# Attention B: a PSUM bank for the values, two weight sets, outputs around the values, and probability squares moved through DRAM

## The chip, the cores and the metric

One Trainium2 chip; the kernel runs on one of its cores. The metric is the device time of one execution in microseconds, the median of several runs. Engines are named as the profile does: PE (TensorE) with its weight loads PEld, DVE (VectorE), ACT (ScalarE), POOL (GpSimd), and SP (SyncE), which here only issues DMAs (SPq in the rows).

## What is computed

Four residual sublayers on x of 8 x 256 tokens x 256 features, all fp32: attention A, a mixture of experts, attention B, and the experts again. The change touches attention B alone:

```
q, k, v = x @ wq, x @ wk, x @ wv        # 16 heads of 128
q, k    = rope(q), rope(k)
s       = (q * mult) @ (k * mult).T     # 256 x 256 per head and sequence, causal mask
p       = softmax(s)
r       = (p @ v) @ wo                  # summed over heads
x       = x + r                         # x had a layernorm ahead of q, k, v
```

## The kernel before, in words

**Precision.** A product in "three parts" (`matmul3`, L114 to L116) splits both factors into a high part (rounded to fp32r) and a low remainder, and runs low x high, high x low, high x high into one accumulation. So every weight has an upper copy made by ACT (`split_hi`, `split_wo`: `wh`, `woh`) and a lower copy made by DVE (`split_lo`, `split_wo`: `wl`, `wol`). In the kernel before there is one set of these four tiles, overwritten for each head pair.

**Tiling.** The 2048 tokens are 4 slots (`s`) of 512 tokens (two sequences each); the 16 heads are 8 head pairs (`it`). A slot of a head pair is the unit of the pipeline, 32 in all, numbered n = 4 it + s. Each has 4 "pairs" j (a head and a sequence), and `step(it, s, j)` is written out by hand for each engine: PE, ACT and DVE run the same 16 steps per head pair in their own fixed order. `moved(it, s, j, by)` names the pair that lies `by` steps later. PE's order in a slot, with n the current slot:

- every j: `scores` of the pair 7 steps ahead, `mix` (probabilities times values) of the pair before
- j = 0: `project` 2 and 3 of slot n+2 (second head's q and k), then `output` 3 of slot n-2
- j = 1: `project_values` 0 of slot n+1
- j = 2: `output` 0 of slot n-1, then `project` 0 and 1 of slot n+3
- j = 3: `project_values` 1 of slot n+1, then `output` 1 and `output` 2 of slot n-1

**PSUM banks.** Scores alternate over banks 0 and 1; `PROJ(i)` is bank 3 or 4 for projection i even or odd; `MIX` has 5 and 6; `OUT` is bank 7 alone. Bank 2 is not used in this stage. The values are projected into `PROJ(0)` and `PROJ(1)` too, so `project_values` waits until the projection before it in that bank was multiplied by the cosines (DVE, `rope`, L378) and copied with swapped halves (ACT, `swap_b`, L372 and L373), and a later `project` waits until the values were copied out (`take_values`, ACT).

**Outputs.** `output(.., t)` (one tile of 128 tokens, both heads, in `OUT`) waits until `add_out` of the tile before it (DVE, two L1235) has read the bank. DVE's order at j = 2 is `row_max` (L1211), `invert`, `turn_squares` (L1221), `add_out` 0, `rope` 0, `rope` 1; at j = 3 it is `row_max`, `invert`, `turn_squares`, `add_out` 1, `mixed_lo`. `add_out` 2 and 3 of a slot follow at j = 0 and 1 of the slot after.

**Rotation.** After `swap`, POOL multiplies by the sines (L378) and adds (L1345), two instructions per projection; `scores` waits for that.

**Weights.** ACT's `split_wo(it)` is at s = 1, j = 0 and DVE's at s = 1, j = 1 of the head pair that uses it from s = 1, j = 2 on. `split_hi` and `split_lo` of the next head pair are at s = 1, j = 1 (q and k, after their last use) and s = 3, j = 0 (values).

**Squares.** `probs` are turned in 32 x 32 squares by DVE (`turn_squares`) within each block of 32 partitions; to be a full transpose the squares must then change partition blocks. SP does this in `move_squares(n)` with 16 DMAs from SBUF to SBUF per slot, each of 32 rows of 1536 bytes. It starts when the four pairs of slot n were turned, which is at j = 1 of slot n-1, and `mix` of slot n, pair 0, which is at j = 1 of slot n, waits for all 16.

PE and ACT run head pairs 1 to 6 in a hardware loop of one head pair; DVE's and SP's steps are written out.

Of the kernel before, what the change touches and what calls it, by code (L numbers as in the profile page):

```python
# [6 lines left out]
ALU = mybir.AluOpType  # L7
# [842 lines left out]
def attention_b(nc, c, name, w_qkv, w_out, stage, wo_stage, stage_in, wo_in, own_norm, norm, ahead):  # L850
# [7 lines left out]
    LANDED = 16 * 16  # L858
    with ExitStack() as ctx:
        sem = lambda n: ctx.enter_context(nc.semaphore(f"{name}_{n}"))  # L860
        sb = lambda n, s, d=F32: ctx.enter_context(nc.sbuf_tensor(f"{name}_{n}", s, d))
        wh, wl = sb("wh", [P, 3, KD, 2 * P], F32R), sb("wl", [P, 3, KD, 2 * P], F32R)
        woh, wol = sb("woh", [P, 2, D], F32R), sb("wol", [P, 2, D], F32R)
# [11 lines left out]
        squares_done, landed = sem("squares_done"), [sem("landed_even"), sem("landed_odd")]  # L875
# [4 lines left out]
        PROJ = lambda i: c.ps[:, 3 + i % 2, :]  # L880
        MIX = lambda h: c.ps[:, 5 + h, :]
# [8 lines left out]
        pair_no = lambda it, s, j: (it * NG + s) * PAIRS + j  # L890
        is_first = lambda it: isinstance(it, int) and it == 0
# [7 lines left out]
        @block.sync  # L899
        def _(sp):  # L900
            def move_squares(n):

                sp.wait_ge(squares_done, PAIRS * (n + 1))
                after(sp, pv_done, PAIRS * (n - 1))
                for qs in range(4):
                    for ks in range(4):
                        sp.dma_start(probsT[ks * SQ:(ks + 1) * SQ, n % 2, qs], squares[qs * SQ:(qs + 1) * SQ, n % 2, ks]).then_inc(landed[n % 2], 16)

            fetch(sp, ahead)
            for it in range(HP):  # L910
                for s in range(NG):
                    move_squares(slot_no(it, s))
                    if s == 0 and it + 1 < HP:

                        sp.wait_ge(w_lo, 2 * (it + 1))
                        sp.dma_start(stage[:], w_qkv[it + 1]).then_inc(stage_in, 16)
                    if s == 3 and it + 1 < HP:

                        sp.wait_ge(wo_lo, it + 1)
                        sp.dma_start(wo_stage[:], w_out[it + 1]).then_inc(wo_in, 16)  # L920

        @block.tensor
        def _(pe):
            def project(it, s, i):
# [5 lines left out]
                early = isinstance(n, int) and n < 2  # L930
                if i == 0:

                    if early:
                        after(pe, rope_read, 3 * n)
                        after(pe, swap_done, 3 * n)
                    else:
                        pe.wait_ge(values_done, 2 * n - 3)
                elif i == 3 and not early:

                    pe.wait_ge(values_done, 2 * n - 2)  # L940
                else:

                    before = (0, 4 * n, 4 * n + 1, 4 * n + 2)[i]
                    after(pe, rope_read, before)
                    after(pe, swap_done, before)
                col = slice((i // 2) * P, (i // 2) * P + P)
                g = slice(s * G, (s + 1) * G)
                for k in range(KD):
                    ins = matmul3(nc, PROJ(i), (wh[:, i % 2, k, col], wl[:, i % 2, k, col]), (c.xh[:, k, g], c.xl[:, k, g]), k == 0, k == KD - 1)
                ins.then_inc(proj_ready, 1)  # L950

            def project_values(it, s, i):
# [12 lines left out]
                for t in range(2):  # L965
                    tok = slice(s * G + (2 * i + t) * P, s * G + (2 * i + t + 1) * P)
                    for k in range(KD):
                        ins = matmul3(nc, PROJ(i)[:, t * 2 * P:(t + 1) * 2 * P], (c.xh[:, k, tok], c.xl[:, k, tok]), (wh[:, 2, k, :], wl[:, 2, k, :]), k == 0, k == KD - 1)
                ins.then_inc(vproj_ready, 1)
# [31 lines left out]
            def output(it, s, t, bank=OUT, before=1):  # L1001
# [14 lines left out]
                for h in range(2):  # L1016
                    ins = matmul3(nc, bank[:, h * D:(h + 1) * D], (mh[:, s % 2, h, tok], ml[:, s % 2, h, tok]), (woh[:, h, :], wol[:, h, :]), True, True)
                ins.then_inc(out_ready, 1)

            def step(it, s, j):  # L1020
# [12 lines left out]
                if j == 0 and not (first and s <= 1):  # L1033
                    output(*moved(it, s, 0, -2 * PAIRS)[:2], 3)
                if j == 2 and not (last and s >= 1):
                    project(*moved(it, s, 0, 3 * PAIRS)[:2], 0)
                    project(*moved(it, s, 0, 3 * PAIRS)[:2], 1)
                if j == 3 and not (first and s == 0):
                    output(*moved(it, s, 0, -PAIRS)[:2], 2)
                if last and s == 3 and j == 0:  # L1040

                    pe.wait_ge(values_done, 2 * NG * HP)
                    norm_turn(nc, c, norm, pe, 0, norm_banks)

            def head_pair(it):
                for s in range(NG):
                    for j in range(PAIRS):
                        step(it, s, j)

            for i in range(4):  # L1050
                project(0, 0, i)
            norm_turn(nc, c, own_norm, pe, 2, own_banks)
            project(0, 1, 0)
            project(0, 1, 1)
            scores(0, 0, 0)
            scores(0, 0, 1)
            project(0, 1, 2)
            project(0, 1, 3)
            scores(0, 0, 2)
            scores(0, 0, 3)  # L1060
            project_values(0, 0, 0)
# [3 lines left out]
            project(0, 2, 0)  # L1065
            project(0, 2, 1)
            scores(0, 1, 0)
            scores(0, 1, 1)
            project_values(0, 0, 1)
# [3 lines left out]
            head_pair(0)  # L1073
            with pe.Fori(1, HP - 1) as it:
                head_pair(it)
            head_pair(HP - 1)
            mix(*LAST)
            output(HP - 1, NG - 2, 3, S(0), 3)
            norm_turn(nc, c, norm, pe, 1, norm_banks)
            output(HP - 1, NG - 1, 0, S(1), 3)  # L1080
            output(HP - 1, NG - 1, 1, OUT, 3)
            output(HP - 1, NG - 1, 2, S(0), 3)
            output(HP - 1, NG - 1, 3, S(1), 3)
# [3 lines left out]
        def _(act):  # L1087
            def split_hi(it, part):
                act.wait_ge(stage_in, 16 * (it + 1))

                if part == 0:
                    after(act, proj_ready, 4 * NG * it)
                else:
                    after(act, vproj_ready, 2 * NG * it)
                nc.scalar.copy(flat(wh[:, parts[part]]), flat(stage[:, parts[part]])).then_inc(w_hi, 1)

            def split_wo(it):
                act.wait_ge(wo_in, 16 * (it + 1))

                after(act, out_ready, TG * NG * it)  # L1100
                nc.scalar.copy(woh[:], wo_stage[:]).then_inc(wo_hi, 1)
# [16 lines left out]
            def take_values(it, s, i):  # L1118
# [4 lines left out]
                nc.scalar.copy(values[:, s % 2, 2 * i:2 * i + 2, :], PROJ(i).rearrange("p (t d) -> p t d", t=2)).then_inc(values_done, 1)  # L1123
# [8 lines left out]
            def step(it, s, j):  # L1132
                first, last = is_first(it), is_last(it)
                if s == 1 and j == 1 and not last:
                    split_hi(it + 1, 0)
                if exists(it, s, j, LEAD):
                    exps(*moved(it, s, j, LEAD))
                if s == NG - 1 and j == 0 and not last:
                    split_hi(it + 1, 1)
# [12 lines left out]
                if s == 1 and j == 0:  # L1152
                    split_wo(it)
# [3 lines left out]
            def head_pair(it):  # L1157
                for s in range(NG):
                    for j in range(PAIRS):
                        step(it, s, j)  # L1160

            split_hi(0, 0)
            split_hi(0, 1)
# [19 lines left out]
            head_pair(0)  # L1183
            with act.Fori(1, HP - 1) as it:
                head_pair(it)
            head_pair(HP - 1)
# [5 lines left out]
        def _(dve):  # L1192
            def split_lo(it, part):
                dve.wait_ge(w_hi, 2 * it + part + 1)
                nc.vector.tensor_tensor(flat(wl[:, parts[part]]), flat(stage[:, parts[part]]), flat(wh[:, parts[part]]).bitcast(F32), ALU.subtract).then_inc(w_lo, 1)

            def split_wo(it):
                dve.wait_ge(wo_hi, it + 1)
                nc.vector.tensor_tensor(wol[:], wo_stage[:], woh[:].bitcast(F32), ALU.subtract).then_inc(wo_lo, 1)
# [37 lines left out]
            def step(it, s, j):  # L1237
# [3 lines left out]
                if s == 1 and j == 1 and not last:  # L1241
                    split_lo(it + 1, 0)
# [7 lines left out]
                if j == 0:  # L1250
                    if s == NG - 1 and not last:
                        split_lo(it + 1, 1)
# [12 lines left out]
                if s == 1 and j == 1:  # L1265
                    split_wo(it)
# [16 lines left out]
            split_lo(0, 0)  # L1283
            norm_rows(nc, c, own_norm, dve, 2)
            split_lo(0, 1)
# [27 lines left out]
            row_max(0, 1, 2)  # L1313
            for it in range(HP):
# [493 lines left out]
```

## Time and profile before

| | us |
|---|---|
| median of 3 runs | 1719.42 (1718.95 to 1720.47) |
| the profiled execution | 1721.0, its span 1719.2 |
| stage of attention B in the span | about 745 to 1430 |

| engine | busy, share of the span | instructions |
|---|---|---|
| PEld | 1334.2 us, 78% | 9400 |
| DVE | 1112.3 us, 65% | 2592 |
| ACT | 816.6 us, 48% | 2012 |
| POOL | 632.2 us, 37% | 550 |

PE, the first engine of the page, has its row further down. Busy time of matmuls overlaps from one to the next, since the end of a matmul is modelled; the start-to-start distance of the rows of a timeline is the better measure of what a matmul costs. The idle time in brackets stands on the first instruction after a gap, with the event that ended it.

### The profile page before, as it was taken

To read this page: it belongs to the slowest core of one execution; us is meant where nothing else is said; L and a number is where in the kernel's file an instruction comes from. 1 tells how busy PE (TensorE), PEld (TensorE's weight loads), DVE (VectorE), ACT (ScalarE), POOL (GpSimd) and SP (SyncE) were. 2 spreads that over 40 slices of the span, in tenths; PEclk is the share of its full clock that TensorE was granted. 3 is DMA by queue.
4 is the path that set the end of the run, shared out by engine and by line. 5 is a ranking of instruction groups with operands and counts; after the bars stand their busy time and mean duration, and the time that the engine had idled before them with its cause. 6 is when DMAs were issued, how large, how long until landed. Compare 5 with 4: busy or idle time off the path is not lost. (4 is left out here: it accounts for less than half of the span.)

```text
span 1719.2 us, 28814 instructions
## 1 busy us (share of the span) xinstructions
PE 1550.6 (90%) x9400; PEld 1334.2 (78%) x9400; DVE 1112.3 (65%) x2592; ACT 816.6 (48%) x2012; POOL 632.2 (37%) x550
## 2 busy tenths in 40 slices
PE   6699999999799999968888888989898878999998
PEld 4588888887688888857777777878787776888887
DVE  6577777777765555664766666666666678655555
ACT  3366666666433333236555555555555633233332
POOL 2676676776100000045555454445454520000000
PEclk9899999999899999989999999999999999999999
DMA  2100000000101000002121221212121210000001
GB/s 90 52 16 16 16 15 15 15 0 1 43 19 37 19 18 0 1 37 56 48 58 49 60 54 45 61 37 63 35 71 35 52 40 31 25 19 19 18 1 49
DMA packets 35232, 57.61 MB, mean 34 GB/s; under 512 B 9280, under 2 KB 29760, under 8 KB 35136
## 3 DMA queue, kind: packets, MB, share of 16 engines
q1 hardware_dynamic: 35136, 56.48, 11.4%
q8 instruction: 42, 0.69, 0.2%
q14 instruction: 54, 0.44, 0.1%
HBM read 29.18 MB, written 2.10 MB: 18 GB/s over the span
## 5 line engine op out<-in xcount | busy, mean ns | idle before, releaser
L378 POOL TENSOR_TENSOR ab_swapped<-ab_swapped,const 128x512 f32<-128x512 f32 x128 | 163.7, 1279 | 289.9 <-ACT ab_swapped L373 289.9
L1626 DVE TENSOR_TENSOR f_hidden<-ps,f_silu 128x512 f32<-128x512 f32 x128 | 87.7, 690 | 202.0 <-PE ps L116 201.9
L1516 ACT ACTIVATE f_silu<-ps 128x512 f32<-128x512 f32 x128 | 76.3, 598 | 283.0 <-PE ps L116 282.9
L114 PE MATMUL ps<-xh,f_wl 128*128 128x512 f32 x512 | 203.2, 397 | 1.5 <-DVE f_hidden L1626 1.5
L115 PE MATMUL ps<-xl,f_wh 128*128 128x512 f32 x512 | 202.8, 396 | 0.0
L116 PE MATMUL ps<-xh,f_wh 128*128 128x512 f32 x512 | 202.6, 396 | 0.0
L1115 ACT ACTIVATE ab_probs<-ab_probs,ab_negmax 128x128 f32<-128x128 f32 (+1 forms) x256 | 114.5, 448 | 151.7 <-DVE ab_negmax L1211 149.1
L1235 DVE SCALAR_TENSOR_TENSOR x<-ps,ab_inv,x 128x256 f32<-128x256 f32 x256 | 121.2, 474 | 88.3 <-PE ps L116 82.0
L1345 POOL TENSOR_TENSOR ab_qk<-ab_qk,ab_swapped 128x512 f32<-128x512 f32 x128 | 170.7, 1333 | 10.0
L73 POOL TENSOR_TENSOR rstd<-shifted,minus_half 128x4 f32<-128x4 f32 x16 | 17.1, 1066 | 358.7 <-DVE shifted L67 358.6
L626 ACT ACTIVATE aa_probs<-ps,aa_negmax 128x256 f32<-128x256 f32 x256 | 119.4, 473 | 59.7 <-DVE aa_negmax L709 52.0
L114 PE MATMUL ps<-f_wh,f_hl 128*128 128x256 f32 x512 | 144.4, 282 | 3.3 <-DVE x L1642 3.3
L709 DVE TENSOR_REDUCE aa_negmax<-ps 128x2 f32<-128x512 f32 x128 | 88.1, 689 | 88.8 <-PE ps L116 87.1
L115 PE MATMUL ps<-f_wl,f_hh 128*128 128x256 f32 x512 | 143.9, 281 | 0.0
L116 PE MATMUL ps<-f_wh,f_hh 128*128 128x256 f32 x512 | 143.9, 281 | 0.0
L114 PE MATMUL ps<-ab_woh,ab_ml 128*128 128x256 f32 x256 | 80.4, 314 | 67.4 <-DVE x L1235 42.1
L378 DVE TENSOR_TENSOR ab_qk<-ps,const 128x512 f32<-128x512 f32 x128 | 87.9, 690 | 70.1 <-PE ps L116 70.1
L372 ACT COPY ab_swapped<-ps 64x512 f32<-64x512 f32 x128 | 74.6, 583 | 101.7 <-DVE ab_qk L378 101.4
L114 PE MATMUL ps<-xh,ab_wl 128*128 128x512 f32 x256 | 111.7, 436 | 11.9 <-ACT ab_swapped L373 5.5
L1211 DVE CUSTOM_DVE_ANT_0 ab_probs<-ps,const 128x128 f32<-128x128 f32 (+1 forms) x256 | 80.9, 355 | 63.5 <-PE ps L980 62.2
L116 PEld LDWEIGHTS ps<-xh,f_wh 128*128 128x128 f32 x512 | 96.3, 188 | 23.3
L1524 ACT CAST f_hh<-f_hidden 128x512 fp32r<-128x512 f32 x128 | 78.8, 617 | 74.8 <-DVE f_hidden L1626 74.8
(187 smaller groups left out, 4564.0 us busy)
## 6 DMA issues: line engine op xcount, KB each, us to landing
ab_probsT<-ab_squares SPq DMA_DIRECT2D x512, 48.0 KB, 1.9
f_stage<-wf_in SPq DMA_DIRECT2D x16, 768.0 KB, 4.2
b_stage<-wb_qkv_in SPq DMA_DIRECT2D x8, 768.0 KB, 4.4
a_stage<-wa_in SPq DMA_DIRECT2D x8, 608.0 KB, 3.8
x<-x_in SPq DMA_DIRECT2D x4, 512.0 KB, 7.2
bo_stage<-wb_out_in SPq DMA_DIRECT2D x8, 256.0 KB, 2.8
out<-x SPq DMA_DIRECT2D x4, 512.0 KB, 2.9
const<-const_in SPq DMA_DIRECT2D x1, 704.0 KB, 5.5
```

The source lines that it names most:

```text
L114: nc.tensor.matmul(out, ll, rh, start=start, stop=False)
L115: nc.tensor.matmul(out, lh, rl, start=False, stop=False)
L116: return nc.tensor.matmul(out, lh, rh, start=False, stop=stop)
L378: return engine.tensor_tensor(by_batch(out), by_batch(src), table(c, rows, col), ALU.mult)
L626: ins = nc.scalar.activation(probs[:, j, q, :], S(j)[:, q * T:(q + 1) * T], ACT.Exp, bias=negmax[:, j, q:q + 1], accum_out=total[:, s % 2, ...
L709: nc.vector.tensor_reduce(negmax[:, j, :], S(j).rearrange("p (q t) -> p q t", q=2), AX, ALU.max, negate=True).then_inc(maxed, 1)
L1115: ins = nc.scalar.activation(probs[:, j, span[q]], probs[:, j, span[q]], ACT.Exp, scale=-1.0, bias=negmax[:, j, q:q + 1], accum_out=total[ ...
L1211: ins = nc.vector.tensor_tensor_reduce(out=probs[:, j, span[q]], in0=S(j)[:, span[q]], in1=mask, scale=-1.0, scalar=3e38, op0=ALU.add, op1 ...
L1235: nc.vector.scalar_tensor_tensor(out=c.x[:, at, :], in0=bank[:, h * D:(h + 1) * D], scalar=inv[:, s, 2 * h + t // 2, t % 2:t % 2 + 1], in1 ...
L1345: nc.gpsimd.tensor_tensor(rows, rows, other, ALU.add).then_inc(rotated, 1)
L1524: nc.scalar.copy(hh[:, s % 2, m, :], hidden[:, m, :]).then_inc(hi_done, 1)
L1626: nc.vector.tensor_tensor(hidden[:, m, :], UP(m), silu[:, m, :], ALU.mult).then_inc(hid_done, 1)
```

## The change

- The values get bank 2 (`VALUES`) and wait only for their own copy-out. `project` waits only for the `rope` and `swap` of the projection two before it.
- All four weight tiles have two halves, used by alternate head pairs. The splits for the next head pair move: ACT at j = 3 of s = 0 (q, k), s = 1 (values), s = 2 (output weights); DVE at the end of j = 1 of s = 1, 2, 3. The first output weights are split ahead of head pair 0. The loop of PE and ACT runs two head pairs per pass, 3 passes instead of 6. The load of the output weights into their stage moves from s = 3 to s = 1.
- PE's order: at j = 2 `project` 0 and 1 go ahead of `output` 0; at j = 3 `output` 1 goes ahead of `project_values` 1. The order of `add_out` and `rope` on DVE stays.
- `move_squares` stores a slot's squares to a DRAM scratch in one DMA (128 rows of 6144 bytes), waits for it, and loads them with 4 DMAs (each 32 partitions x 4 runs of 1536 bytes). `turn_squares` waits for the store of two slots ago, not for the landing.

```diff
+        VALUES = c.ps[:, 2, :]
...
                 sp.wait_ge(squares_done, PAIRS * (n + 1))
+                after(sp, landed[n % 2], LANDED * (n // 2))
+                sp.dma_start(scratch[n % 2], squares[:, n % 2].rearrange("p b k j i -> p (b k j i)")).then_inc(written[n % 2], 16)
+
+                sp.wait_ge(written[n % 2], 16 * (n // 2 + 1))
                 after(sp, pv_done, PAIRS * (n - 1))
-                for qs in range(4):
-                    for ks in range(4):
-                        sp.dma_start(probsT[ks * SQ:(ks + 1) * SQ, n % 2, qs], squares[qs * SQ:(qs + 1) * SQ, n % 2, ks]).then_inc(landed[n % 2], 16)
+                rows = scratch[n % 2].rearrange("(a p) (b f) -> b p a f", a=4, b=4)
+                for b in range(4):
+                    sp.dma_start(probsT[b * SQ:(b + 1) * SQ, n % 2].rearrange("p a k j i -> p a (k j i)"), rows[b]).then_inc(landed[n % 2], 16)
...
+                after(pe, rope_read, 4 * n + i - 1)
+                after(pe, swap_done, 4 * n + i - 1)
...
-                before = (4 * n + 7, 4 * n + 10)[i]
-                before = min(before, ROPES) if isinstance(before, int) else before
-                pe.wait_ge(rope_read, before)
-                pe.wait_ge(swap_done, before)
-
-                after(pe, values_done, 2 * n - 1 + i)
+                after(pe, values_done, 2 * n + i)
...
                 if j == 0 and not (last and s >= NG - 2):
-                    project(*moved(it, s, 0, 2 * PAIRS)[:2], 2)
-                    project(*moved(it, s, 0, 2 * PAIRS)[:2], 3)
-                if j in (1, 3) and not (last and s == NG - 1):
-                    project_values(*moved(it, s, 0, PAIRS)[:2], j // 2)
+                    for i in (2, 3):
+                        project(*later(it, half, s, 2), i)
+                if j == 1 and not (last and s == NG - 1):
+                    project_values(*later(it, half, s, 1), 0)
+                if j == 0 and not (first and s <= 1):
+                    output(*later(it, half, s, -2), 3)
+                if j == 2 and not (last and s >= 1):
+                    for i in (0, 1):
+                        project(*later(it, half, s, 3), i)
                 if j >= 2 and not (first and s == 0):
-                    output(*moved(it, s, 0, -PAIRS)[:2], j - 2)
...
+                    output(*later(it, half, s, -1), j - 2)
+                if j == 3 and not (last and s == NG - 1):
+                    project_values(*later(it, half, s, 1), 1)
                 if j == 3 and not (first and s == 0):
-                    output(*moved(it, s, 0, -PAIRS)[:2], 2)
+                    output(*later(it, half, s, -1), 2)
...
-                after(dve, landed[s % 2], LANDED * (2 * it + s // 2))
+                after(dve, written[s % 2], 16 * (2 * it + s // 2))
...
+                if s >= 1 and j == 1 and not last:
+                    if s < NG - 1:
+                        split_lo(it + 1, 1 - it % 2, s - 1)
+                    else:
+                        split_wo(it + 1, 1 - it % 2)
```

## Rows read from the trace of the kernel before

**Rows 1.** The page's busy time by engine: busy us, share of span, instructions.

```profile
PE 1550.6 (90%) x9400; PEld 1334.2 (78%) x9400; DVE 1112.3 (65%) x2592; ACT 816.6 (48%) x2012; POOL 632.2 (37%) x550
```

**Rows 2.** Busy by stretch: length, PE, PEld, DVE, ACT, POOL; PEclk, DMA share, GB/s.

```profile
845.00:864.00 19.00, 17.17 (x105) 15.32 (x106) 12.89 (x39) 11.36 (x30) 10.35 (x9) 1.00 0.23 58
899.00:910.00 11.00, 9.00 (x44) 7.58 (x44) 5.68 (x19) 5.36 (x14) 5.03 (x4) 0.84 0.28 69
```

**Rows 3.** PE's timeline, j=2 and j=3: start, duration, line, tiles, [idle before, releaser].

```profile
938.80 0.36 PE L114 MATMUL ps<-ab_woh,ab_ml 128*128 128x256 f32 x1
...
939.57 0.40 PE L114 MATMUL ps<-xh,ab_wl 128*128 128x512 f32 x1
...
942.39 0.82 PE L980 MATMUL ps<-ab_qk 128*128 128x128 f32 x4
943.04 0.59 PE L998 MATMUL ps<-ab_probsT,ab_values 128*128 128x256 f32 x2
...
944.58 0.36 PE L114 MATMUL ps<-ab_wh,xl 128*128 128x256 f32 x1 [0.72 <-issue]
...
946.10 0.28 PE L114 MATMUL ps<-ab_woh,ab_ml 128*128 128x256 f32 x1
...
948.06 0.38 PE L114 MATMUL ps<-ab_woh,ab_ml 128*128 128x256 f32 x1 [1.10 <-DVE x L1235]
...
948.87 0.82 PE L980 MATMUL ps<-ab_qk 128*128 128x128 f32 x4
```

**Rows 4.** PE's timeline: one weight stall per head pair, and the values' second part.

```profile
820.35 0.36 PE L114 MATMUL ps<-ab_woh,ab_ml 128*128 128x256 f32 x1 [3.38 <-DVE ab_wol L1199]
...
882.65 0.36 PE L114 MATMUL ps<-ab_wh,xl 128*128 128x256 f32 x1 [0.73 <-issue]
...
899.51 0.38 PE L114 MATMUL ps<-ab_woh,ab_ml 128*128 128x256 f32 x1 [3.59 <-DVE ab_wol L1199]
...
963.44 0.36 PE L114 MATMUL ps<-ab_wh,xl 128*128 128x256 f32 x1 [0.72 <-issue]
...
1372.83 0.36 PE L114 MATMUL ps<-ab_wh,xl 128*128 128x256 f32 x1 [0.72 <-issue]
```

**Rows 5.** DVE's timeline: a split of 1024 columns, ropes, an output's add, a row maximum.

```profile
894.74 2.01 DVE L1195 TENSOR_TENSOR ab_wl<-b_stage,ab_wh 128x1024 fp32r<-128x1024 f32 x1 [1.52 <-ACT ab_wh L1095]
...
933.70 1.33 DVE L378 TENSOR_TENSOR ab_qk<-ps,const 128x512 f32<-128x512 f32 x2
...
939.77 1.00 DVE L1235 SCALAR_TENSOR_TENSOR x<-ps,ab_inv,x 128x256 f32<-128x256 f32 x2
...
943.24 0.29 DVE L1211 CUSTOM_DVE_ANT_0 ab_probs<-ps,const 128x128 f32<-128x128 f32 x1
...
943.88 0.56 DVE L1221 STREAM_TRANSPOSE ab_squares<-ab_probs 128x384 f32<-128x384 f32 x1
...
947.00 1.00 DVE L1235 SCALAR_TENSOR_TENSOR x<-ps,ab_inv,x 128x256 f32<-128x256 f32 x2 [2.56 <-PE ps L116]
```

**Rows 6.** Timelines of ACT and POOL: second half of swap 1, last add of rotation 1.

```profile
943.91 0.58 ACT L373 COPY ab_swapped<-ps 64x512 f32<-64x512 f32 x1
...
947.18 1.27 POOL L1345 TENSOR_TENSOR ab_qk<-ab_qk,ab_swapped 128x512 f32<-128x512 f32 x1
```

**Rows 7.** DMA issues, KB each, median us to landing; then one slot's sixteen issues.

```profile
ab_probsT<-ab_squares SPq DMA_DIRECT2D x512, 48.0 KB, 1.9
...
b_stage<-wb_qkv_in SPq DMA_DIRECT2D x8, 768.0 KB, 4.4
...
out<-x SPq DMA_DIRECT2D x4, 512.0 KB, 2.9
...
L907 SPq DMA_DIRECT2D ab_probsT<-ab_squares x16: 507/591/1482, 936.9 to 947.2; - x16
```

**Rows 8.** PE's timeline ahead of the first steps: two gaps of the prologue.

```profile
779.60 0.48 PE L114 MATMUL ps<-xh,ab_wl 128*128 128x512 f32 x1 [1.23 <-ACT ab_values L1123]
...
795.94 1.22 PE L998 MATMUL ps<-ab_probsT,ab_values 128*128 128x256 f32 x2 [4.79 <-DMA ab_probsT<-ab_squares]
```

More of the change, by code:

```diff
@@ L890, in attention_b @@
         pair_no = lambda it, s, j: (it * NG + s) * PAIRS + j
+        later = lambda it, half, s, by: (it + (s + by) // NG, half ^ ((s + by) // NG % 2), (s + by) % NG)
         is_first = lambda it: isinstance(it, int) and it == 0
@@ L923, in _, with project @@
         def _(pe):
-            def project(it, s, i):
+            def project(it, half, s, i):
                 n = slot_no(it, s)
@@ L999, in mix, with output @@
                 nc.tensor.matmul(out[:, P:T], v(1), columns(slice(2, 3)), start=False, stop=True).then_inc(pv_done, 1)
-            def output(it, s, t, bank=OUT, before=1):
+            def output(it, half, s, t, bank=OUT, before=1):
                 n = slot_no(it, s)
@@ L1040, in step, with head_pair @@
                 if last and s == 3 and j == 0:
-                    pe.wait_ge(values_done, 2 * NG * HP)
+                    pe.wait_ge(swap_done, ROPES)
                     norm_turn(nc, c, norm, pe, 0, norm_banks)
-            def head_pair(it):
+            def head_pair(it, half):
                 for s in range(NG):
                     for j in range(PAIRS):
-                        step(it, s, j)
+                        step(it, half, s, j)
             for i in range(4):
-                project(0, 0, i)
+                project(0, 0, 0, i)
@@ L1062, in _ @@
             norm_turn(nc, c, own_norm, pe, 3, own_banks)
             pe.wait_ge(own_norm.lo_done, KD * (NG - 1))
-            project(0, 2, 0)
-            project(0, 2, 1)
+            project(0, 0, 2, 0)
+            project(0, 0, 2, 1)
             scores(0, 1, 0)
             scores(0, 1, 1)
-            project_values(0, 0, 1)
+            project_values(0, 0, 0, 1)
             scores(0, 1, 2)
             pe.wait_ge(own_norm.lo_done, KD * NG)
-            head_pair(0)
-            with pe.Fori(1, HP - 1) as it:
-                head_pair(it)
@@ L1076, in _ @@
-            head_pair(HP - 1)
+            head_pair(0, 0)
+            with pe.Fori(0, HP // 2 - 1) as two:
+                head_pair(2 * two + 1, 1)
+                head_pair(2 * two + 2, 0)
+            head_pair(HP - 1, 1)
             mix(*LAST)
-            output(HP - 1, NG - 2, 3, S(0), 3)
+            output(HP - 1, 1, NG - 2, 3, S(0), 3)
             norm_turn(nc, c, norm, pe, 1, norm_banks)
-            output(HP - 1, NG - 1, 0, S(1), 3)
-            output(HP - 1, NG - 1, 1, OUT, 3)
@@ L1122, in take_values @@
                 after(act, pv_done, PAIRS * (n - 1))
-                nc.scalar.copy(values[:, s % 2, 2 * i:2 * i + 2, :], PROJ(i).rearrange("p (t d) -> p t d", t=2)).then_inc(values_done, 1)
+                nc.scalar.copy(values[:, s % 2, 2 * i:2 * i + 2, :], VALUES.rearrange("p (t d) -> p t d", t=2)).then_inc(values_done, 1)
             def mixed_hi(it, s, h):
@@ L1130, in mixed_hi, with step @@
                 nc.scalar.copy(mh[:, s % 2, h, :], MIX(h)).then_inc(mix_hi, 1)
-            def step(it, s, j):
+            def step(it, half, s, j):
                 first, last = is_first(it), is_last(it)
-                if s == 1 and j == 1 and not last:
-                    split_hi(it + 1, 0)
                 if exists(it, s, j, LEAD):
                     exps(*moved(it, s, j, LEAD))
-                if s == NG - 1 and j == 0 and not last:
-                    split_hi(it + 1, 1)
+                if s == 0 and j == 3 and not last:
+                    split_hi(it + 1, 1 - half, 0)
+                if s == 1 and j == 3 and not last:
+                    split_hi(it + 1, 1 - half, 1)
+                if s == 2 and j == 3 and not last:
+                    split_wo(it + 1, 1 - half)
                 if j == 0 and not (first and s == 0):
@@ L1182, in _ @@
             exps(0, 1, 2)
[L1183 to L1186, printed above, removed]
+            split_wo(0, 0)
+            head_pair(0, 0)
+            with act.Fori(0, HP // 2 - 1) as two:
+                head_pair(2 * two + 1, 1)
+                head_pair(2 * two + 2, 0)
+            head_pair(HP - 1, 1)
             mixed_hi(HP - 1, NG - 1, 1)
```

98 lines of the change are left out of this document (38 added, 60 removed).

## The prediction, made before the changed kernel was run

> **What bounds the kernel now.** I read the page's busy times first: PE is busy 90% of the span, DVE 65%, the others under half [rows 1]. In a stretch of one undisturbed slot of attention B PE is busy 17.17 of 19 us, DVE 12.89, ACT 11.36 and POOL 10.35 [rows 2], so PE sets the pace and only its gaps and its own work count. PE's timeline gives the gaps. The values' second part comes round at 944.58 and 963.44: a slot takes 18.86 us [rows 3, 4]. It holds two gaps. Ahead of `project_values` 1, PE should go on at 943.62 (`mix` takes 0.58) and starts at 944.58: 0.96 us. It waits for `swap` 1, whose second half ends at 944.49 [rows 3, 6]; the trace says only "issue". Ahead of `output` 2, PE should go on at 946.80 (`output` 1 is six matmuls of 0.117, 0.70) and starts at 948.06: 1.26 us, for DVE's `add_out` 1, which starts at 947.00 [rows 3, 5]. Third, once per head pair PE waits 3.59 us for the lower output weights (899.51) [rows 4], whose DVE split is queued behind another split of 2.01 us, itself waiting for ACT [rows 5]; right behind it the granted clock is 0.84 over 11 us [rows 2], that is the lower level (1.2 of 2.4 GHz) for part of the stretch after the idle time. From the values' part in s = 0 of head pair 1 (882.65) to that of head pair 7 (1372.83) are 490.18 us, 81.70 per head pair [rows 4]. Four slots of 18.86 are 75.44; 3.59 plus some 0.1 of slow start is the stall; the remaining 2.6 is the clock. This stage is 40% of the kernel; nothing else is changed.
>
> **The values' own bank.** `project_values` 1 no longer waits for `swap` 1. What it now waits for, the copy-out of the values before, happened half a slot earlier. -0.96 per slot. A bank that was idle is used, nothing is added.
>
> **The weights' second set.** The same splits run elsewhere. On DVE they go to the end of j = 1. Is there room? At j = 2 DVE is now to wait for an `output` 0 that ends 4.8 us after that step's scores start; its own work ahead of that takes some 2.0 (943.24 to 943.88 plus 0.5 is 1.1, from 0.85 after the scores [rows 3, 5]), so 2.8 us are idle and the 2.01 us split fits in. ACT's split at j = 3 delays `take_values` 1 by about 1 us, needed by PE only at j = 1 of the next slot. So zero; without that cover it would be 2.0 us per head pair. The stall of 3.6 goes, and the dip of 2.6 with it, since the gaps of up to 1.26 that remain show no dip now (clock 1.00 over a whole slot with both [rows 2]). -6.2 per head pair where it exists, bounds 3.6 and 6.6.
>
> **The output order.** Here is the step where a stall does not just go. Let t0 be the end of `output` 0. PE then needs: scores 0.65, mix 0.58, `output` 1 0.77 (938.80 to 939.57), values 1.43 (1.52 less 0.09, since they no longer follow a mix) [rows 3]: `output` 2 could start at t0 + 3.43. DVE's order did not change, and `output` 0 now ends behind `project` 0 and 1, so both ropes are queued behind its `add_out`. DVE: `add_out` 0 starts at t0 + 0.20 (939.77 against 939.57) and holds it 0.92; two ropes take 1.31; `row_max`, `invert` and the transpose 1.12; so `add_out` 1 starts at t0 + 3.55. From its start to `output` 2's first matmul are 1.06 (947.00 to 948.06) [rows 3, 5]: t0 + 4.61. A stall of 1.2 us replaces the one of 1.26. `output` 1 itself would start at t0 + 1.23 and its add is through at t0 + 1.26: nothing. The new slot: from `scores` of j = 3 to the next `scores` was 6.48 (942.39 to 948.87) and becomes 4.61 + 0.81 = 5.42; the other three steps hold the same instructions without gaps, j = 2 in another order. So 18.86 - 6.48 + 5.42 = 17.80.
>
> **Who else is behind the later ropes.** `swap` 0 and 1 now end at t0 + 3.0 and t0 + 4.3, where the old `swap` 1 ended 2.1 after the scores of j = 3. PE's next `project` 3 in that bank starts at t0 + 8. POOL's last add ended 6.06 after those scores (947.18 + 1.27) [rows 6] and so ends at about t0 + 8.2; the scores that need it are at t0 + 5.4 + 4.8 = 10.2. 2 us of cover, no cost. If these ropes came 2 us later still, PE would stall one for one.
>
> **The squares.** Sixteen issues on SP went from 936.9 to 947.2, and the last lands 1.9 later, 949.1 [rows 7]. `mix` of j = 1 is a slot after the one at about 935.5, at 954.3: 5.2 us of slack now. In the new slot the chain may last 16.4 us from 936.9 on. Its price: the store is not in the trace. Nearest rows: 512 KB stored to DRAM land after 2.9, 768 KB loaded after 4.4 [rows 7]; I take 4.4, the same size. Four loads: three issues of about 0.6 ahead of the last, which lands after 1.9 (48 KB) to 4.4 (768 KB, all four together), so 3.7 to 6.2. With 0.9 for a slow first issue (1482 against 591 ns): 7.5 to 11.5, I take 10. Hidden in 16.4. SP's wait for the store has behind it only the four loads and a weight load that has a whole slot. The waits on the weights in SP's program are all satisfied earlier than before. If nothing overlapped, four loads at 4.4 each and the store would be 22 + 0.9, 6.5 too late: the upper bound.
>
> The loads now read DRAM in runs of 1536 bytes. The only runs of that size here are SBUF to SBUF, and no run here shows such a load from DRAM. The Trainium skill (Perfetto Trace Analysis, DMA Optimizations) says that DMAs under 2 KB have significant overhead per transfer, and (DMA: Bandwidth & Descriptors, Anatomy of one DMA) that completion waits most of all on the receipt of the write, heaviest into HBM. By that rule the chain would be longer than by the rows; it gives no number for this shape, and bears on the rival below. The trace agrees in part: 1.9 us for 48 KB into SBUF, 2.9 for 512 KB into DRAM [rows 7], where size explains the difference as well.
>
> **Ends of the stage.** Prologue: `project` (0, 2, 0) no longer waits 1.23 for the values [rows 8], which moves the first squares up by perhaps 0.7; the first `mix` waits 4.79 for their DMAs, a chain of 11.4 us that becomes about 10, bounds 7.5 and 16. -3, bounds 0 and -4, as PE has little else to do. Head pair 0: 0.96 in s = 0, 1.06 in each of s = 1 to 3, and the stall of 3.38 [rows 4]: -7.6. Head pair 7: 1.06 in s = 0; in s = 1 and 2 there are no ropes at j = 2, so `add_out` 1 is in time and 1.2 each go, less what DVE's normalisation takes back: -3, bounds 0 and -4.
>
> **The sum.** 24 slots: 490.2 - 24 x 17.80 = 490.2 - 427.2 = -63.0. With -3, -7.6 and -3: -76.6. The profiled execution (1721.0, span 1719.2) lies 1.6 above the median of 1719.42, within the sum's error. 1719.4 - 76.6 = 1642.8, I say 1643.
>
> **Rivals.**
> First, 1643 as above, 0.60. Own range 1630 to 1655.
> Second, the stall at `output` 2 vanishes too, because DVE gets to `add_out` 1 over a microsecond earlier than I reckon. Then 26 slots gain 1.2 more: 1612. For it: the balance is of two sums of 3 to 4 us each. Against: every term has a row. 0.08.
> Third, a further wait of 0.5 to 1.5 us per slot turns up: `scores` for POOL (cover 2 us), ACT at j = 3 with exps, split and values copy in one queue, or DRAM loads that take 17 us. Times 28 slots: 1657 to 1685, say 1670. For it: ropes, swaps and rotations are all moved 2 us later at once, and five engines' waits are newly placed. 0.23.
> Fourth, the other side: the squares' chain through DRAM sets the slot. The slot is then 1.4 us (the transpose against the mix) plus the chain. It decides from 16.4 us and makes the kernel slower than before once the chain passes 81.70/4 - 1.4 = 19.0 us. With the serial price of 22.9 the slot is 24.3, 6.5 above 17.8, times 28: 1643 + 182 = 1825. Against: all 16 DMA engines were shared by one 48 KB DMA at a time at a mean share of 0.2 to 0.3 [rows 2], and 768 KB in one DMA take 4.4. A chain between 17 and 19 is in the third case. 0.05 for slower, and 0.04 for a chain that about cancels or halves the gain (1690 to 1719).
>
> **How the numbers follow.** The time is that of the first case. The second is left out below but for its edge, the fourth above: 1622 to 1680 leaves out about 0.06 below and 0.12 above. 0.2% of the time is 3.4 us, about what a measurement can tell from no change. Faster by more 0.93, within 0.02, slower 0.05.
>
> **What would show it.** A slot of PE of 17.8 us (`output` 2 to `output` 2) with one gap of about 1.0 to 1.2 ahead of `output` 2, released by DVE's add to `x`, and none ahead of the values; no gap for `ab_wol` and clock 1.00 from 810 on; DVE with both ropes right behind `add_out` 0 in a row, and idle some 1 to 3 us ahead of that; store and last load done some 10 us after the fourth transpose. Wrong would make it: a DMA as the releaser of `mix`, POOL as that of `scores`, or a slot much off 17.8.

## The result, and the profile after

The changed kernel takes 1657.89 us (median of 4 runs, 1656.41 to 1659.81) against 1719.95 us before (median of 4), a ratio of 0.964 (95% interval 0.9624 to 0.9657): 62 us less, where 76.6 less were forecast (1643, range 1622 to 1680). The profiled execution of the changed kernel took 1657.26, its span is 1655.4.

The page's busy times, which answer to [rows 1]: PE's share went from 90 to 93%, with the same 9400 matmuls.

```profile
PE 1532.2 (93%) x9400; PEld 1322.7 (80%) x9400; DVE 1102.1 (67%) x2592; ACT 813.9 (49%) x2012; POOL 637.6 (39%) x550
```

PE's timeline of the changed kernel, one row for each kind of gap and those that bound the stretches below (start us, duration, line, tiles, [idle before, what ended it]). They answer to [rows 3, 4, 8].

```profile
742.59 1.09 PE L92 MATMUL ps<-const,normed 128*128 128x128 f32 x8 [2.12 <-DVE normed L81]
...
790.85 1.22 PE L987 MATMUL ps<-ab_probsT,ab_values 128*128 128x256 f32 x2 [3.02 <-DMA ab_probsT<-ab_scratch]
...
872.20 0.39 PE L114 MATMUL ps<-ab_woh,ab_ml 128*128 128x256 f32 x1 [0.79 <-DVE x L1229]
883.12 0.47 PE L114 MATMUL ps<-xh,ab_wl 128*128 128x512 f32 x1 [1.08 <-DVE ab_wl L1189]
891.15 0.39 PE L114 MATMUL ps<-ab_woh,ab_ml 128*128 128x256 f32 x1 [0.77 <-DVE x L1229]
908.78 0.39 PE L114 MATMUL ps<-ab_woh,ab_ml 128*128 128x256 f32 x1 [0.77 <-DVE x L1229]
...
944.00 0.39 PE L114 MATMUL ps<-ab_woh,ab_ml 128*128 128x256 f32 x1 [0.79 <-DVE x L1229]
...
998.19 0.38 PE L114 MATMUL ps<-ab_woh,ab_ml 128*128 128x256 f32 x1 [0.79 <-DVE x L1229]
1002.48 1.65 PE L969 MATMUL ps<-ab_qk 128*128 128x128 f32 x4 [3.34 <-issue]
1022.15 0.39 PE L114 MATMUL ps<-ab_woh,ab_ml 128*128 128x256 f32 x1 [0.77 <-DVE x L1229]
...
1093.97 0.38 PE L114 MATMUL ps<-ab_woh,ab_ml 128*128 128x256 f32 x1 [0.77 <-DVE x L1229]
...
1152.15 1.65 PE L969 MATMUL ps<-ab_qk 128*128 128x128 f32 x4 [3.06 <-issue]
1170.47 0.39 PE L114 MATMUL ps<-ab_woh,ab_ml 128*128 128x256 f32 x1 [0.79 <-DVE x L1229]
...
1314.13 0.39 PE L114 MATMUL ps<-ab_woh,ab_ml 128*128 128x256 f32 x1 [0.77 <-DVE x L1229]
...
1367.96 0.77 PE L1421 MATMUL ps<-xl,wr 128*128 128x512 f32 x1 [2.90 <-PEq L859]
```

The reader is to see four things. `output` 2 comes round every 17.6 us (891.15, 908.78, and so on), with a gap in front of it and none in front of the values. The stall of 3.59 for `ab_wol` is gone. A stall for `ab_wl` of 1.08 us is new, once per head pair (883.12). And new are two gaps, of 3.34 and 3.06 us, put down to "issue", at 1002.48 and 1152.15; in the program both stand where PE's loop of two head pairs jumps back to its start (behind head pairs 2 and 4).

The same places in the kernel before, from PE's timeline, to measure the stretches against:

```profile
744.13 1.09 PE L92 MATMUL ps<-const,normed 128*128 128x128 f32 x8 [2.12 <-DVE normed L81]
...
886.09 0.39 PE L114 MATMUL ps<-ab_woh,ab_ml 128*128 128x256 f32 x1 [1.10 <-DVE x L1235]
...
1376.31 0.38 PE L114 MATMUL ps<-ab_woh,ab_ml 128*128 128x256 f32 x1 [1.10 <-DVE x L1235]
...
1432.63 0.47 PE L1427 MATMUL ps<-xl,wr 128*128 128x512 f32 x1 [2.90 <-PEq L859]
```

| stretch | before | after | change | forecast |
|---|---|---|---|---|
| start of the stage to the first `mix` | 51.81 | 48.26 | -3.6 | -3 |
| to `output` 2 in s = 0 of head pair 1 | 90.15 | 81.35 | -8.8 | -8.7 (head pair 0 and a slot) |
| 24 slots, to the same in head pair 7 | 490.22 | 441.93 | -48.3 | -63.0 |
| to the first logits of the experts | 56.32 | 53.83 | -2.5 | -2 |

The whole difference to the forecast lies in the 24 slots. From the rows: 24 slots of 17.62 are 422.9; 944.00 less 872.20 is 71.80, 1.3 over four slots, and six such surpluses are 7.9; head pairs 2 and 4, which end at a jump, take 78.15 and 76.50, 6.35 and 4.70 more. 422.9 + 7.9 + 11.05 = 441.9, what was measured.

The windows at the jump (length, then busy PE, PEld, DVE, ACT, POOL; granted clock, DMA share, GB/s) show the price's second half: behind the gap the granted clock is at its lower level (1.2 of 2.4 GHz) for up to 6 us. From 872 to 944 us, a head pair with its gaps of 0.8 and 1.1, it is 1.00.

```profile
872.00:944.00 72.00, 67.62 (x416) 60.65 (x416) 51.15 (x157) 44.55 (x117) 42.47 (x33) 1.00 0.34 103
...
1002.00:1004.00 2.00, 1.52 (x5) 1.35 (x6) 0.00 (x0) 0.00 (x0) 0.10 (x1) 0.50 0.03 8
...
1006.00:1008.00 2.00, 2.00 (x6) 1.55 (x5) 0.25 (x1) 0.30 (x1) 0.00 (x0) 0.50 0.00 0
```

DVE's timeline of the changed kernel: the new split, then the chain between two outputs, which answers to [rows 5].

```profile
881.29 1.58 DVE L1189 TENSOR_TENSOR ab_wl<-b_stage,ab_wh 128x1024 fp32r<-128x1024 f32 x1
...
904.54 1.00 DVE L1229 SCALAR_TENSOR_TENSOR x<-ps,ab_inv,x 128x256 f32<-128x256 f32 x2 [2.15 <-PE ps L116]
905.46 1.28 DVE L378 TENSOR_TENSOR ab_qk<-ps,const 128x512 f32<-128x512 f32 x2
906.65 0.28 DVE L1205 CUSTOM_DVE_ANT_0 ab_probs<-ps,const 128x128 f32<-128x128 f32 x1
...
907.76 0.96 DVE L1229 SCALAR_TENSOR_TENSOR x<-ps,ab_inv,x 128x256 f32<-128x256 f32 x2
```

`add_out` 0, two ropes right behind it, the row maximum, the transpose, `add_out` 1 at 907.76, and `output` 2 at 908.78: the order that was forecast. DVE is idle 2.15 us ahead of it.

SP's timeline for one slot, and the page's DMA issues (KB each, median us to landing), against [rows 7]:

```profile
916.49 0.34 SPq L908 DMA_DIRECT2D ab_scratch<-ab_squares  x1
919.76 2.09 SPq L914 DMA_DIRECT2D ab_probsT<-ab_scratch  x4
```

```profile
ab_scratch<-ab_squares SPq DMA_DIRECT2D x32, 768.0 KB, 3.3
ab_probsT<-ab_scratch SPq DMA_DIRECT2D x128, 192.0 KB, 3.8
...
b_stage<-wb_qkv_in SPq DMA_DIRECT2D x8, 768.0 KB, 5.8
```

The store takes 3.3 us, the four loads are issued within 2.1, and the last lands some 3.8 after its issue: about 9 us where 10 were taken and sixteen DMAs took 12.2. No `mix` but the first waits for a DMA.

### The profile page after: what moved, and what is told of

Read it like the earlier page. It is cut to its first block and busy times, and to the rows that moved or that the text cites. A ratio compares the mean times of both kernels' runs of the same rounds, so it can differ in the third digit from the quotient of the medians.

```text
span 1655.4 us, 28360 instructions
## 1 busy us (share of the span) xinstructions
PE 1532.2 (93%) x9400; PEld 1322.7 (80%) x9400; DVE 1102.1 (67%) x2592; ACT 813.9 (49%) x2012; POOL 637.6 (39%) x550
## 5 line engine op out<-in xcount | busy, mean ns | idle before, releaser
L1339 POOL TENSOR_TENSOR ab_qk<-ab_qk,ab_swapped 128x512 f32<-128x512 f32 x128 | 175.2, 1369 | 10.0
L114 PEld LDWEIGHTS ps<-xh,f_wl 128*128 128x128 f32 x512 | 96.4, 188 | 23.0 <-DVE f_hidden L1620 2.4
L969 PE MATMUL ps<-ab_qk 128*128 128x128 f32 (+1 forms) x512 | 106.6, 333 | 7.2 <-issue 6.4
```

The costliest lines, as they stand in the source:

```text
L114: nc.tensor.matmul(out, ll, rh, start=start, stop=False)
L969: ins = nc.tensor.matmul(S(j)[:, span[q]], qk[:, s % 2, 2 * h, b * T + q * P:b * T + (q + 1) * P], qk[:, s % 2, 2 * h + 1, b * T:b * T + ( ...
L1339: nc.gpsimd.tensor_tensor(rows, rows, other, ALU.add).then_inc(rotated, 1)
```

## The experiments

Each is an edit of the changed kernel or of the kernel before; the times of the kernel before beside them were 1719.35 to 1720.06.

**1. The jump.** PE's head pairs written out.

```diff
-            with pe.Fori(0, HP // 2 - 1) as two:
-                head_pair(2 * two + 1, 1)
-                head_pair(2 * two + 2, 0)
+            for it in range(1, HP - 1):
+                head_pair(it, it % 2)
```

> The changed kernel, with PE's head pairs 1 to 6 written out instead of a loop of two head pairs (ACT keeps its loop). Theory: the two waits of 3.3 us put down to 'issue', at 1002 and 1152 us, are PE's own, at the jump back to the loop's start; without the jump they and the half clock behind them go, 6.35 and 4.7 us by the distance of the same output in two head pairs: 1657.9 - 11 = 1647. Rival: they are waits for another engine (POOL's add ends 0.3 us before both), or for ACT, which loops too: 1658, unchanged.

1647.57 us (ratio to before 0.9576, 0.9560 to 0.9592): 10.3 less than the changed kernel. What PE waited for between 850 and 1330 us (total us, times, longest) has no "issue" any more; POOL and ACT run as before, ACT still in its loop:

```profile
PE ps L114 <- DVE x L1228: 22.1, 28, 1.5
PE ps L114 <- DVE ab_wl L1188: 5.2, 6, 0.9
PE ps L969 <- POOL ab_qk L1338: 0.5, 1, 0.5
```

So the gaps belong to PE's own jump, not to POOL or ACT.

**2. The same jump in the kernel before.**

```diff
-            with pe.Fori(1, HP - 1) as it:
-                head_pair(it)
+            with pe.Fori(0, HP // 2 - 1) as two:
+                head_pair(2 * two + 1)
+                head_pair(2 * two + 2)
```

> The kernel before, with PE's loop over two head pairs per pass instead of one, nothing else changed. Theory: it is the length of the loop's body that makes the jump cost something; two gaps of about 3.3 us appear that the loop of one head pair does not have, 1720 + 7 to 11 = 1729. Rival: the gap comes with the new order or the two weight sets: 1720, no gap.

1732.73 us (1.0073, 1.0056 to 1.0089): 12.7 slower than before. PE's timeline has the gap twice, where the loop of one head pair jumps five times and shows none of that kind:

```profile
1035.47 1.64 PE L980 MATMUL ps<-ab_qk 128*128 128x128 f32 x4 [4.50 <-issue]
...
1206.38 1.65 PE L980 MATMUL ps<-ab_qk 128*128 128x128 f32 x4 [4.69 <-issue]
```

The length of the body makes the difference, not the order of the change. The pages' lists of DMA queues (packets, MB, share) show the code being loaded: in the kernel before

```profile
q8 instruction: 42, 0.69, 0.2%
```

and in this one

```profile
q8 instruction: 64, 1.05, 0.3%
```

Only PE's loop differs between the two, so the 22 more packets of 16 KB on this queue are PE's instructions. In the kernel before it has none at all from 955 to 1320 us, where the loop runs on; in this one it has nine from the first jump to the second (1031 to 1202 us), the first of them in the gap, between 1032 and 1033. (The changed kernel has 64 packets too, and 59 with PE written out.) The short body is loaded once and kept, and the long one is loaded anew in each pass. That PE waits for that one packet is the likely reading of the gap; the profile names no releaser.

The Trainium skill (Runtime: NRT & Kernel Launch, Instruction fetch mechanics) says that a taken branch to a target outside the window of instructions held at the time must fetch it before it goes on. The trace agrees: loads on every pass and a stall at the jump with the long body, and with the short one neither once its first pass is over. A head pair is 416 matmuls and as many weight loads, 832 instructions without the waits, and two are 1664. The same page of the Trainium skill gives PE room for 2048 instructions; that would, as an estimate, hold either body without its waits, so the figure does not tell them apart. The runs do not show where between one and two head pairs the limit lies.

**3. The gap ahead of `output` 2.**

```diff
+                if j == 2 and not (last and s >= 1):
+                    rope(*moved(it, s, 0, 3 * PAIRS)[:2], 0)
+                    rope(*moved(it, s, 0, 3 * PAIRS)[:2], 1)
                 if j >= 2 and not (first and s == 0):
                     add_out(*moved(it, s, 0, -PAIRS)[:2], j - 2)
...
-                if j == 2 and not (last and s >= 1):
-                    rope(*moved(it, s, 0, 3 * PAIRS)[:2], 0)
-                    rope(*moved(it, s, 0, 3 * PAIRS)[:2], 1)
```

> The changed kernel, with DVE's two ropes at j = 2 ahead of add_out 0 instead of behind it, in PE's own order. Theory: the gap ahead of output 2 (0.77 us idle, 1.0 by the starts) is the ropes in front of add_out 1; it goes, the slot falls from 17.62 to 16.6 us, 25 slots: 1657.9 - 25 = 1633. Rival: another wait is right behind (output 1 for add_out 0, scores for row_max), so half or less of it: 1645 or more.

1627.08 us (0.9457, 0.9442 to 0.9473): 30.8 less than the changed kernel, more than the 25 expected. DVE's timeline shows the second `rope` ahead of `add_out` 0, and `add_out` 1 2.05 us behind `add_out` 0 instead of 3.22:

```profile
916.97 0.69 DVE L378 TENSOR_TENSOR ab_qk<-ps,const 128x512 f32<-128x512 f32 x1 [0.71 <-PE ps L116]
917.68 1.00 DVE L1229 SCALAR_TENSOR_TENSOR x<-ps,ab_inv,x 128x256 f32<-128x256 f32 x2
...
919.73 1.00 DVE L1229 SCALAR_TENSOR_TENSOR x<-ps,ab_inv,x 128x256 f32<-128x256 f32 x2
```

No gap for `x` is left on PE in the 24 slots. The stall that the prediction placed is the one that stood there. The gain is larger than expected because the gap stood in 28 slots, not 25, and cost 1.09 in each, not 1.0 (a head pair is 67.43 here, with the wait for `ab_wl` still in it, against 71.80).

**4. The wait for the query and key weights.**

```diff
+                    if s == 1 and not last:
+                        split_lo(it + 1, 1 - it % 2, 0)
...
-                if s >= 1 and j == 1 and not last:
+                if s >= 2 and j == 1 and not last:
                     if s < NG - 1:
-                        split_lo(it + 1, 1 - it % 2, s - 1)
+                        split_lo(it + 1, 1 - it % 2, 1)
```

(The added lines stand at j = 0, behind the ropes.)

> The changed kernel, with DVE's split of the next query and key weights at the end of j = 0 of s = 1 instead of the end of j = 1. Theory: project 0 of the next head pair (s = 1, j = 2) waits for that split, 1.08 us idle once per head pair and 1.3 by the period; it goes: 1657.9 - 7 x 1.2 = 1649.5. Rival: the split now delays row_max and add_out 3 in j = 1 and the wait only moves: 1656 to 1658.

1649.40 us (0.9594, 0.9578 to 0.9610): 8.5 less. The outputs come round every 17.63 us through a whole head pair, s = 1 included; three of them, that of s = 1 at 889.92:

```profile
872.29 0.39 PE L114 MATMUL ps<-ab_woh,ab_ml 128*128 128x256 f32 x1 [0.77 <-DVE x L1229]
889.92 0.39 PE L114 MATMUL ps<-ab_woh,ab_ml 128*128 128x256 f32 x1 [0.77 <-DVE x L1229]
907.56 0.39 PE L114 MATMUL ps<-ab_woh,ab_ml 128*128 128x256 f32 x1 [0.77 <-DVE x L1229]
```

**5. The order taken out.** The changed kernel with PE's old order.

```diff
+                if j == 3 and not (last and s == NG - 1):
+                    project_values(*later(it, half, s, 1), 1)
+                if j >= 2 and not (first and s == 0):
+                    output(*later(it, half, s, -1), j - 2)
...
                 if j == 2 and not (last and s >= 1):
                     for i in (0, 1):
                         project(*later(it, half, s, 3), i)
-                if j >= 2 and not (first and s == 0):
-                    output(*later(it, half, s, -1), j - 2)
-                if j == 3 and not (last and s == NG - 1):
-                    project_values(*later(it, half, s, 1), 1)
```

> The changed kernel, with PE's old order (output 0 ahead of project 0 and 1; project_values 1 ahead of output 1). Theory: the order alone brings little, since a wait of 1.0 stands where one of 1.26 stood: the slot is 18.86 - 0.96 = 17.90 instead of 17.62, 26 slots: +7, and -3 where project 0 now comes 0.7 us later and finds the weights split (7 times 0.4): 1662 to 1665. Rival: the order is what removes the waits: slots of 18.8, 1690.

1660.47 us (0.9654, 0.9637 to 0.9670): 2.6 slower, beside runs that scatter by 3. Two rows of PE, 17.89 us apart, with the old gap of 1.10 ahead of `output` 2:

```profile
908.35 0.39 PE L114 MATMUL ps<-ab_woh,ab_ml 128*128 128x256 f32 x1 [1.10 <-DVE x L1229]
926.24 0.39 PE L114 MATMUL ps<-ab_woh,ab_ml 128*128 128x256 f32 x1 [1.10 <-DVE x L1229]
```

The new order of PE by itself brought 0.27 us per slot, less what `project` 0 lost by coming earlier (`ab_wl` is waited for 0.37 here, 1.08 there).

**6. The squares' new way taken out.** The changed kernel with the sixteen transfers of before in `move_squares` (the lines with a minus in the diff of the change, and `LANDED` 16 x 16).

> The changed kernel, with the squares moved as before (16 DMAs from SBUF to SBUF, no DRAM). Theory: the move is hidden in either form; its chain is 9.1 us through DRAM and 12.2 with sixteen, with 16.2 us to spare in a slot; only the first mix of the stage sees it, so 1658 to 1661. Rival: SP's queue or the DMAs' traffic matter in the faster slots: 1665 or more, or under 1655.

1660.78 us (0.9658, 0.9642 to 0.9675): 2.9 slower. The first `mix` starts 2.3 us later than in the changed kernel, and no other waits for a DMA:

```profile
793.16 1.22 PE L982 MATMUL ps<-ab_probsT,ab_values 128*128 128x256 f32 x2 [5.64 <-DMA ab_probsT<-ab_squares]
```

**7. The values' bank alone.** The kernel before with `VALUES` in bank 2 and the changed kernel's waits in `project` and `project_values`.

```diff
+        VALUES = c.ps[:, 2, :]
...
+                after(pe, rope_read, 4 * n + i - 1)
+                after(pe, swap_done, 4 * n + i - 1)
...
+                after(pe, values_done, 2 * n + i)
```

> The kernel before, with the values in bank 2 and the waits of project and project_values that go with it, nothing else. Theory: 0.96 us per slot go, 28 slots, and 1 to 2 in the prologue: 1720 - 28 = 1692. Rival: the wait at output 2 grows by as much, since DVE is not ahead: 1710 to 1720.

1684.77 us (0.9800, 0.9784 to 0.9817): 35 less than before, 7 more than expected. PE's timeline:

```profile
878.70 0.39 PE L114 MATMUL ps<-ab_woh,ab_ml 128*128 128x256 f32 x1 [1.10 <-DVE x L1218]
892.12 0.57 PE L114 MATMUL ps<-ab_woh,ab_ml 128*128 128x256 f32 x1 [3.59 <-DVE ab_wol L1182]
...
955.45 0.38 PE L114 MATMUL ps<-ab_woh,ab_ml 128*128 128x256 f32 x1 [1.10 <-DVE x L1218]
```

A slot is 17.88 us in that timeline, 0.98 less. A head pair (878.70 to 955.45) is 76.75 where it was 81.70 (mean): 3.92 of that is the slots, the other 1.0 is in the slow stretch behind the `ab_wol` stall, which is as long as before (3.59) but is mostly followed by less time at the lower clock: by the windows some 3.0 us behind the stall of head pair 1 and 3.4 behind that of head pair 2, where it was 3.4 and 5.7 in the kernel before. Six times 1.0 is most of what was not expected.

**8. The weight sets alone,** with all that comes with them, the longer loop too: the changed kernel with the edits of 5 and 6 and the values in `PROJ` with their old waits.

> The changed kernel without the values' bank, without the new order and with the sixteen DMAs, so that only the two weight sets, their moved splits and the loop of two head pairs are left. Theory: the stall at the lower output weights and the half clock behind it go, 6.2 in each of 6 head pairs and 3.4 in the first, 41 in all; the loop's jumps cost 11 to 13, the wait for the split of the query and key weights up to 3: 1720 - 41 + 14 = 1693. Rival: the half clock stays (it comes with the stage, not with the stall): 1708.

1694.91 us (0.9855, 0.9839 to 0.9872), 24.4 less than before.

```profile
863.60 0.39 PE L114 MATMUL ps<-ab_woh,ab_ml 128*128 128x256 f32 x1 [1.10 <-DVE x L1242]
...
939.56 0.38 PE L114 MATMUL ps<-ab_woh,ab_ml 128*128 128x256 f32 x1 [1.10 <-DVE x L1242]
...
1021.29 1.22 PE L982 MATMUL ps<-ab_qk 128*128 128x128 f32 x3 [4.83 <-issue]
```

A head pair without a jump is 75.96 us, 5.7 less than 81.70; the gap at the jump is there with this part alone. The two parts put into the kernel before bring 35 and 24.4, the two taken out of the changed kernel cost 2.6 and 2.9. The sum of 65 makes the 62 of the whole within the scatter of the runs, which is as large as either of the last two.

**9. The three edits together** (1, 3 and 4).

> The changed kernel with three edits together: PE's head pairs written out, DVE's ropes ahead of add_out 0, DVE's split of the next query and key weights one step earlier. Theory: the three waits lie one behind the other on PE, so their gains add: 1657.9 - 10.3 - 30.8 - 8.5 = 1608.3, and a slot of 16.5 us without a gap. Rival: in the shorter slot another wait appears (POOL's rotation for scores, or the split in front of add_out 3): 1615 or more.

1609.18 us (median of 5; 0.9354, 0.9341 to 0.9368): the gains add to within 1 us. It is 48.7 us faster than the changed kernel and 110.6 faster than before. Four slots of it in the view by windows:

```profile
860.00:926.00 66.00, 66.00 (x415) 60.02 (x414) 52.26 (x155) 44.70 (x115) 42.03 (x32) 1.00 0.39 112
```

PE is busy all of the 66 us at the full clock, 16.5 per slot.

**10 and 11. The point from which the chain through DRAM decides.** Each slot's squares stored three and four times, one after the other, before they are loaded.

```diff
-                sp.dma_start(scratch[n % 2], squares[:, n % 2].rearrange("p b k j i -> p (b k j i)")).then_inc(written[n % 2], 16)
-
-                sp.wait_ge(written[n % 2], 16 * (n // 2 + 1))
+                for again in range(4):
+                    sp.dma_start(scratch[n % 2], squares[:, n % 2].rearrange("p b k j i -> p (b k j i)")).then_inc(written[n % 2], 16)
+                    sp.wait_ge(written[n % 2], 64 * (n // 2) + 16 * (again + 1))
```

> The changed kernel, in which each slot's squares are stored to DRAM three times, one after the other, before they are loaded. The chain from the last transpose to the last landing is 8.8 us with one store of 3.3 and becomes 15.4. Theory: a slot of 17.6 us leaves 16.2; still hidden, only the first mix of the stage is 6.5 us later: 1664. Rival: any longer chain or more traffic costs in every slot: over 1680.

> The changed kernel, in which each slot's squares are stored to DRAM four times before they are loaded. The chain becomes 18.6 us, over the 16.2 that a slot leaves. Theory: mix waits for the landing in each slot, the slot is 1.4 + 18.6 = 20.0 us instead of 17.6, about 29 slots, and 10 us in the prologue: 1658 + 70 + 10 = 1738. Rival: there is more slack than reckoned, and it costs only the prologue: 1668.

1678.6 us with three (0.9761, 0.9742 to 0.9779) and 1747.0 with four (1.0159, 1.0139 to 1.0178), the median of two runs each. The second is 9 us above its expectation; the first missed its by 15. SP's timeline of the kernel with three stores, in one slot, says why:

```profile
889.13 8.59 SPq L909 DMA_DIRECT2D ab_scratch<-ab_squares  x3
900.65 1.75 SPq L914 DMA_DIRECT2D ab_probsT<-ab_scratch  x4
```

From the first store to the first load are 11.5 us. The stores are not alike: from each to the next step on SP are 3.4, 4.9 and 3.3 us. In about half of the slots each takes 3.3 and the three take 9.8, as in the slot from 962.7; in most of the others one of them takes up to 5.1, and the three up to 11.6 (at the two ends of the stage 12.1 to 15.3). Why one is slow was not traced. With some 5.3 for the loads (their last issue and its landing) the chain is 15.1 in the first kind, what was expected, and up to 16.9 in the second, over the 16.2 that a slot leaves. So it costs in some slots, and not in every one as the rival had it. PE waited for it, beside the first `mix` (10.0), nine times and 8.5 us in all in that run. With four stores the wait is 68.1, the first `mix` (13.1) counted in (total us, times, longest):

```profile
PE ps L987 <- DMA ab_probsT<-ab_scratch: 18.5, 10, 10.0
```

```profile
PE ps L987 <- DMA ab_probsT<-ab_scratch: 68.1, 18, 13.1
```

Both runs fit the limit of about 16 us. In two slots of the timeline four stores take 13.0 and 15.3, which makes chains of 18.3 and 20.6 us, and the kernel is slower than before, as the fourth rival has it from 19.0 on; the change's own chain of 9 is far below. Of the 14 us of experiment 10 that are not the first `mix`, 8.5 are shown as waits for the DMA and 1.4 as longer gaps at the jumps (7.8 against 6.4); the rest was not traced further.

## Why the prediction was right, and where its sum was not

**The bound and the three stalls: right.** PE set the pace. Experiments 7, 8 and 3 take away the stall for the values, the one for `ab_wol` and the one at `output` 2, one by one.

**The values' bank: right in mechanism, 0.96 forecast, 0.98 measured** per slot; alone it brings 35 us.

**The output order: right in mechanism, the stall a little over-sized.** "A stall of 1.2 us replaces the one of 1.26": it measures 1.0 by the starts (PE could go on at 907.85, 0.12 behind the start of the last matmul at 907.73, and starts at 908.78, which is 0.93, and 0.1 of slow start come on top). The slot was forecast at 17.80 and is 17.62. The chain on DVE from the end of `output` 0 took 4.4 instead of 4.61, mostly since two ropes in a row cost 1.19, not 1.31. Experiment 3 shows that the ropes' place in DVE's queue is the cause.

**The weights' second set: one step failed.** "So zero", for DVE's split at the end of j = 1, looked at who waits on DVE behind it and not at who waits for its result. `project` 0 of the next head pair is at j = 2 of s = 1 in PE's new order, right behind: the split ends at 882.87 and PE starts at 883.12, after 1.08 us of idle time. 1.3 us in each of six head pairs are 7.9 us; experiment 4 gets 8.5 back.

**The loop: a step that was missing.** The prediction names nothing for the loop of two head pairs, though it is in the diff. Two jumps cost 6.35 and 4.70 us, 3.34 and 3.06 of it as gaps and the rest as matmuls at the lower clock; experiment 1 gets 10.3 back, and experiment 2 puts 12.7 on the kernel before. The trace of before shows five jumps without a gap, so a price could be bounded from it only at zero; the length of the body was what the trace could not tell.

**The clock: right in mechanism.** It is 1.00 from 810 to 998 us, as forecast, where the stall for `ab_wol` is gone. The forecast counted that gain and not that the gaps of 3.34 and 3.06 at the jumps would bring 0.50 back behind them.

**The squares: right.** A chain of 9 us for 10, hidden, with -3.6 for -3 in the prologue, of which 2.3 are the transfers (experiment 6). The rule that the prediction set beside its rows, by which this chain would come out longer, did not show: the four loads in runs of 1536 bytes landed after 3.8, within the 1.9 to 4.4 of the rows, and the store into DRAM after 3.3, less than the 4.4 taken.

The terms: -63.0 + 7.9 (the split) + 11.05 (the jumps) - 24 x 0.18 (the shorter slot) = -48.4, measured -48.3. The other stretches came out within 1.5 us of their forecast in all. So of the 14.9 us by which 1643 was missed, the two steps are 19, and the slot gave 4 back.

**How much of it was luck.** 1657.9 lies 3 us outside the first case's own range (1630 to 1655) and at the near end of the third's (1657 to 1685). The third named a wait of 0.5 to 1.5 us in every slot, for POOL, for ACT or for the loads. None of these happened: PE waits for POOL once, behind the 24 slots (0.5 us at 1325), and the 19 us are a wait once per head pair and two jumps. So the stated range held the result because other waits had been allowed for, and not because these two were seen, and the over-sized slot hid 4 us of them.

## What to carry to other kernels

A step that is moved has two sides: who is queued behind it, and who waits for what it makes. When an order changes on one engine, write down for each product of a moved step how far its first reader is now. And where a change makes a hardware loop's body longer, the jump itself may begin to cost: look for a gap put down to "issue" at the place of the jump, and count the clock behind it too.

## What the runs showed of the hardware that was not expected

- A loop of one head pair on PE (832 matmuls and weight loads) jumps back without a gap, and loads no code while it runs (no packet on the instruction queue q8 from 955 to 1320 us); one of two head pairs loads it anew in each pass (nine packets of 16 KB in experiment 2), stalls 3.1 to 4.8 us at each jump (changed kernel, experiments 2 and 8), and then runs up to 6 us at a granted clock of 0.50.
- Idle times of 0.8 to 1.1 us of PE did not move the granted clock (1.00 from 872 to 944 us); behind those of 3.1 to 4.8 at the jumps it was 0.50.
- A store of 768 KB to DRAM landed after 3.3 us, quicker than a load of that size before the change (4.4). A load of that size beside the new traffic took 5.8.
- Three such stores, each issued when the one before had landed, took 9.8 us in some slots (3.3 each) and up to 11.6 in most others, where one of the three took up to 5.1.
